# A place of its own in the written order for each step of a pair of batches, in a two-layer mixer with routed experts

## The reference

```python
for layer in (0, 1):
    xn = (x - mean(x)) / sqrt(var(x) + 1e-5)
    if layer == 0:
        xx = shift(xn) - xn                              # the token before, less this one
        mix = tanh((xn + xx * maa_x) @ w1)               # 5 groups of 32
        xw, xk, xv, xr, xg = (xn + xx * (maa[i] + mix[i] @ w2[i]) for i in range(5))
        r, k, v, g = xr @ Wr, xk @ Wk, xv @ Wv, silu(xg @ Wg)
        w = time_decay + tanh(xw @ d1) @ d2
        # per head, over time: y = r (S + u k v^T);  S = exp(-exp(w)) S + k v^T
        s = (groupnorm(y) * g) @ Wo
        f = sum over the 2 best of 8 experts: p_e * W3[e] (silu(xn W1[e]) * (xn W2[e]))
    else:
        s = concat_heads(softmax(q k^T / sqrt(8)) v) @ W_out
        f = shared(xn) + sum over the 2 best of 8 experts: expert_e(sigmoid(score_e) * xn)
    x = x + s * silu(f)
```

## Time and profile before

| what | value |
| --- | --- |
| median of 3 runs | 2736.35 us (2729.3 to 2741.03) |
| span of the profiled execution | 2756.3 us, 50388 instructions |
| TensorE, matmuls | 2327.5 us busy, 84% of the span |
| TensorE, weight loads | 1579.5 us, 57% |
| VectorE | 1609.7 us, 58% |
| ScalarE | 1350.3 us, 49% |
| GpSimd | 1237.6 us, 45% |
| 16 transfer engines | 31% of their time, 90 GB/s |

### The profile page before, as it was taken

How to read it: one execution, slowest core, us unless ns; L and a number is a source line. 1 busy time by engine, 2 the same in 40 slices (tenths; PEclk the granted TensorE clock), 3 DMA queues, 4 the chain that set the end, 5 groups by cost and what they waited for, 6 DMA issues and landing times. The chain is left out here.

```text
span 2756.3 us, 50388 instructions
## 1 busy us (share of the span) xinstructions
PE 2327.5 (84%) x16602; PEld 1579.5 (57%) x16602; DVE 1609.7 (58%) x3864; ACT 1350.3 (49%) x2485; POOL 1237.6 (45%) x1364
## 2 busy tenths in 40 slices
PE   1666889898998989898898989889898889998785
PEld 1553556566665656566565656556565656665363
DVE  2336465766657475665657465665647566665452
ACT  0222555455554546545554545545554555555453
POOL 3144435364633645444732646435643646323503
PEclk5768899999999999999999999999999999999897
DMA  3320223323333333323332333324333332321132
GB/s 104 111 75 12 68 91 95 106 73 111 98 100 89 99 99 99 94 77 111 101 103 82 99 93 97 107 75 121 100 90 93 96 102 85 110 72 41 53 107 68
DMA packets 308767, 248.27 MB, mean 90 GB/s; under 512 B 31040, under 2 KB 300064, under 8 KB 308512
## 3 DMA queue, kind: packets, MB, share of 16 engines
q1 hardware_dynamic: 292128, 211.46, 25.7%
q0 software_dynamic: 16384, 33.59, 4.1%
HBM read 195.77 MB, written 48.10 MB: 88 GB/s over the span
## 5 line engine op out<-in xcount | busy, mean ns | idle before, releaser
L1445 DVE TENSOR_REDUCE rowmax<-bank_s 128x1 f32<-128x512 f32 x1016 | 698.5, 687 | 565.6 <-PE bank_s L887 542.3
L1063 ACT ACTIVATE probs<-bank_st 128x512 f32<-128x512 f32 x992 | 589.4, 594 | 462.7 <-PE bank_st L902 431.9
L902 PE MATMUL bank_st<-qs,ks 128*128 128x512 f32 x992 | 512.6, 517 | 59.3 <-ACT probs L1063 58.0
L887 PE MATMUL bank_s<-ks,qs 128*128 128x512 f32 x1016 | 448.6, 442 | 93.8 <-DVE rowmax L1445 84.9
L1207 POOL DMA_INDIRECT yg<-ys_d,index x256 | 249.8, 976 | 260.7 <-issue 242.1
L902 PEld LDWEIGHTS bank_st<-qs,ks 128*128 128x128 f32 x992 | 191.5, 193 | 234.5 <-ACT probs L1063 140.6
L887 PEld LDWEIGHTS bank_s<-ks,qs 128*128 128x128 f32 x1016 | 197.0, 194 | 207.4 <-DVE rowmax L1445 173.6
L1329 DVE SCALAR_TENSOR_TENSOR hid<-hid,bank_h 128x512 f32<-128x512 f32 x224 | 148.6, 664 | 223.7 <-ACT hid L984 216.7
L916 PE MATMUL bank_pv<-probs,v 128*32 128x512 f32 x2048 | 253.8, 614 | 0.8 <-ACT probs L1063 0.8
L728 PEld LDWEIGHTS bank_h<-xT_sb,wbuf 128*128 128x128 f32 x1472 | 202.6, 202 | 27.9 <-issue 14.6
L1125 POOL TENSOR_TENSOR pause_sb<-ones_sb,power_sb 128x8 f32<-128x8 f32 x128 | 214.2, 1674 | 3.9
(11 more groups left out here) (245 smaller groups left out, 3659.4 us busy)
## 6 DMA issues: line engine op xcount, KB each, us to landing
wbuf<-up SPq DMA_DIRECT2D x368, 128.0 KB
wbuf<-gate SPq DMA_DIRECT2D x368, 128.0 KB
wbuf<-down SPq DMA_DIRECT2D x368, 128.0 KB
xs_sb<-xs_d SPq DMA_DIRECT2D x80, 256.0 KB
ys_d<-y_sb SPq DMA_DIRECT2D x80, 256.0 KB
xn<-x SPq DMA_DIRECT2D x16, 256.0 KB, 3.2
x<-x SPq DMA_DIRECT2D x16, 256.0 KB, 4.1
yg<-ys_d,index POOLq DMA_INDIRECT x256
```

What stands on the lines that cost most here:

```text
L887: mm(room(s, b)[:], qs[:, slot, q * P:(q + 1) * P], ks[:, slot, j, :], start=True, stop=True).then_inc(filled[b], 1)
L902: mm(room(s, b)[:], ks[:, slot, j, k * P:(k + 1) * P], qs[:, slot, :], start=True, stop=True).then_inc(filled[b], 1)
L1063: A(probs[:, tile % PRING, :], ps[:], ACT.Exp).then_inc(emptied[b], 1)
L1445: v.reduce_max(rowmax[:, h // HG % 2, NT * (h % HG) + q:NT * (h % HG) + q + 1], content(s, b)[:], AX).then_inc(emptied[b], 1)
```

## The change

Two tables are added, and two functions that read them. `MOVED` gives each single step of a pair of batches a number that is added to its due time on all engines: the key is the batch within the pair, the layer and the kind, and the list has one entry for each step of that kind. A second and a third dictionary hold what is added on top for the first and the last pair. `SHIFTED` adds a shift for each engine, layer and kind, again with an extra for the first and the last pair. `DRIFT` adds 0.0006 for each batch. The numbers in `MOVED` are mostly between -1 and 1, with some between -5 and 6; whole rows of layer 1's `gather`, `scatter` and `stack` move together. Nothing else is changed: the instructions, their operands, the banks and the waits are the same, but for the fill counts that are worked out from the new order.

```diff
-    return PERIOD * n + at
+    return PERIOD * n + at + moved(step)
+
+
+DRIFT = 0.0006
+MOVED = (
+    {
...
+        (1, 0, "wkvT"): [2.35], (1, 0, "wkvsum"): [-0.18], (1, 0, "yn"): [0.04],
...
+    },
...
+)
+SHIFTED = {
...
+    "dve": {
...
+        (1, "gate"): (-0.08, 0, 0), (1, "gather"): (-0.28, 0, 0), (1, "keys"): (-0.37, 0, 0), (1, "mrow"): (-0.02, 0, 0), (1, "normT"): (0.35, 0, 0),
...
+}
+
+
+def class_of(n):
+
+    return 1 if n < DUO else 2 if n >= B - DUO else 0
+
+
+def among(table, n, key, i, otherwise):
+
+    at = table[0].get(key, otherwise)[i]
+    return at + table[class_of(n)].get(key, otherwise)[i] if class_of(n) else at
+
+
+PLACES = [{} for i in range(DUO)]
+for places, steps in zip(PLACES, DUE):
+    for s in sorted(steps):
+        kin = [t for t in sorted(steps) if t[:2] == s[:2]]
+        places[s] = (kin.index(s), [0.0] * len(kin))
+
+
+def moved(step):
+
+    n = step[0]
+    i, still = PLACES[n % DUO][step[1:]]
+    return DRIFT * n + among(MOVED, n, (n % DUO, *step[1:3]), i, still)
+
+
+def shifted(engine, step):
+
+    every, *ends = SHIFTED[engine].get(step[1:3], (0, 0, 0))
+    return every + (ends[class_of(step[0]) - 1] if class_of(step[0]) else 0)
...
-    return sorted(PLAN, key=lambda s: due(s) + LATER[engine].get(s[2], 0.0))
+    return sorted(PLAN, key=lambda s: due(s) + LATER[engine].get(s[2], 0.0) + shifted(engine, s))
```

109 lines of the change are left out of this document (added).

## The result

The changed kernel takes 2609.87 us (median of 4 runs, 2604.09 to 2613.72) against 2732.82 us before (4 runs on the same chip, 2722.59 to 2741.03). The ratio is 0.9552, with a 95% interval of 0.9527 to 0.9577: 123 us less where 69 were forecast.

The account below looks back on a forecast made before the run. TensorE's idle time, 33.8 us a pair, bounds the kernel; 1.5 + 1.7 + 7.0 + 2.4 - 2.7 = 9.9 us a pair, times 7 is 69 off the 2736.35 median: 2670 us predicted, range 2622 to 2728 (8 in 10).

Parts of the forecast that it names:

- The row maximum behind combine: VectorE's queue: with wkvT behind the reduction, TensorE's 1.58 us bank_s wait goes; 1.5 us a pair.
- decay: ScalarE's queue: tanh ahead of two keys or an exponential shortens TensorE's wait between decay's halves; 1.7 us a pair.
- Short returns of the two banks: TensorE's order: fewer bank_s and bank_st matmuls follow their predecessor too soon; 7.0 us a pair, 4.9 visible.
- Places of other kinds: xT ahead of headsT, VectorE's statistics earlier, row maxima ahead of small operations; 2.4 us a pair.
- New waits: TensorE: one in 20 of 86 moved steps waits 0.6 us for its input; 2.7 us a pair back.
- the wait for wkvT: TensorE at L865: a new wait there would show the forecast wrong; wkvT was expected to fit by 0.3 us.
- GpSimd and SyncE at nothing: Norm behind three gathers, scatters, decays, lora and SyncE issues change places; costed at nothing, nothing gained.
- Half a pair for the start, 2 us for the end: Half a pair's gain added to 6.5 for the filling; the last 211.7 us left unchanged to 2 us.
- So there is little to be had: TensorE's granted clock, 0.98 in the six pairs, is nearly all at its upper level, so little gain there.
- The rule on the ports: VectorE and GpSimd lock shared SBUF ports: the collision moves to L1355, 0.6 us new wait a pair, 2674 us.
- more than is counted: Rival: an engine freed sooner frees its next bank sooner; 15 to 17 us a pair, 2617 to 2631; chance 0.13.
- the first rival: Waits only change place between the engines' queues; net under 2 us a pair, 2722 to 2736; chance 0.10.

Follow-up runs that it names:

- e13: The kernel before, unchanged, run again for a second profiled execution: 2731.26 us, ratio 1.0006.
- e9: The kernel before with only wkvT of each odd batch's layer 0 moved 2.35 us later: 2729.41 us, ratio 0.9983.
- e18: The changed kernel with only the move of wkvT in odd batches undone: 2610.52 us, ratio 0.9566.
- e10: The kernel before with only layer 0's decay moved earlier on ScalarE, ahead of keys and exponentials: 2728.86 us, ratio 0.9983.
- e5: The changed kernel with ScalarE's queue without its shifts: 2639.92 us, ratio 0.9657.
- e6: The changed kernel with VectorE's queue without its shifts: 2641.56 us, ratio 0.9674.
- e8: The changed kernel with the queues of GpSimd and SyncE without their shifts: 2625.05 us, ratio 0.961.
- e15: The changed kernel with both tables for layer 1 alone, layer 0 as before: 2723.30 us, ratio 0.9971.
- e3: The changed kernel with one table for all pairs, without extras for the first and last pair: 2612.15 us, ratio 0.9568.
- e11: The kernel before with matmuls of ones in TensorE's waits inside decay and for the norm of even batches: 2730.84 us, ratio 0.999.
- e17: e8 with three matmuls of ones ahead of the wait for mixin's input in even batches: 2623.68 us, ratio 0.9613.
- e16: The kernel before with the single moves of wkvT and of decay together: 2722.62 us, ratio 0.9976.

## Why the prediction was right or wrong

Right: what bounds the kernel (TensorE's idle time among the two banks), the sign, and what the places named look like afterwards. Wrong: the size, 9.9 us a pair where 19.1 came. The sum, sorted by what a trace can show (the 7.0 us of short returns count as 4.9 of waits and 2.1 of overlap, as the forecast split them):

| us a pair | forecast | measured, e13 against after |
|---|---|---|
| waits for the two banks, combine's included | 6.4 | 8.5 |
| waits inside decay | 1.7 | 1.6 |
| waits of other kinds | 2.4 | 3.1 |
| new waits, charged on top | -2.7 | none beyond what the three rows above are already net of |
| TensorE's busy time | 2.1 | 6.1 |

So the mechanism was right and three sizes were off: the short returns of the banks, the new waits, and above all the busy time, 4.0 of the 9.2 us missing. By the steps of the forecast:

- *The row maximum behind combine, 1.5 us.* The wait of 1.58 went and the add runs in 0.69, as said. As a term of a sum it fails: alone it gave under half (e9), and in the changed kernel its undoing costs nothing that the runs can tell (e18).
- *decay, 1.7 us.* Sized right as a wait: 1.6 us, 2.2 left where 2.1 was said. Alone it came back as 1.8 us of `bank_s` (e10).
- *Short returns of the two banks, 7.0 us, 4.9 of them visible.* This is the term that was mis-sized. The visible waits for the two banks fell by 8.5 us a pair, 7.0 of them without combine's. By starts of matmuls, the time that TensorE spends from each `soft` to its next matmul fell from 0.460 to 0.418 us, 5.3 us in 128, and from each `smax` by 5.5 us a pair: 10.8 us, where the two terms together had 8.5. The count looks at TensorE's row only and misses what the release of a bank waits for in the other two queues. The experiments refute it as a measure: e5, e6 and e8 have the count of the changed kernel and are 15 to 32 us slower, and e15 has a count 4.4 us worse than before and is faster.
- *Places of other kinds, 2.4 us.* A little too low; it is 3.1 net. The waits for the norm (1.5 us a pair), for the transfer of the experts' input (1.0) and for the transposed heads (0.8) are no longer in the list.
- *New waits, 2.7 us back.* They came, and more than said: 5.0 us a pair in front of 66 matmuls in six pairs, eleven a pair where four or five were taken. They are on the two banks (39 of the 66), at `bank_y` (0.5 us a pair), at the transposes behind `gT` (0.3) and at the router (0.2); one, of 0.6 us, is the wait for wkvT that the forecast named as a sign of being wrong. What the forecast missed is that 19.0 us of waits went against them. The count of short returns is net of most of this, so that charging 2.7 on top of it was the mistake: it is 19 of the missing 54 us.
- *GpSimd and SyncE at nothing.* Right for the norm behind three gathers, which no longer waits 9.77 us and delays nobody; wrong for the queues as a whole (e8, 15 us).
- *Half a pair for the start, 2 us for the end.* The 123 us are 6.5 pairs of 19.1, where the forecast took 7 and up to 2 us; 3.9 and 4.9 of them lie before and behind the six pairs. The tables of the first and last pair play no part that shows (e3).
- *"So there is little to be had" from the clock.* This was put at nearly nothing, and the runs don't bear it out. The lost clock went from 4.3 to 0.3 us a pair. In e11 and e17, 2.4 and 3.4 us less of it took 2.2 and 2.7 us off TensorE's busy time without the fillers. The pair became only 0.5 and 1.1 us shorter, but the fillers had put TensorE back by 1.35 and 1.4 us. If that delay counts in full, the clock gave about 1.8 and 2.5 us, and 4.0 us less lost clock would be worth about 3 of the 19.1; if it cost nothing, about 1. This is an estimate between two bounds; the timed runs (3.0 and 1.4 us) can't be told from nothing. The rest of the 6.1 us of busy time, about half, is in records that overlap more where the queue flows, as the forecast had it with 2.1. I infer that from the rows and haven't shown it apart.
- *The rule on the ports (the Trainium skill, "SBUF — State Buffer", section "SBUF: two separate sides").* The 1.41 us add beside GpSimd's subtraction became 0.69 without it, so far the trace agrees. The 0.6 us of new wait behind L1355 didn't come. That isn't against the page, which gives the ports to whichever of the two starts first: L1506 (the same line, now) starts 0.22 us before the subtraction, is overlapped by it for 0.47 us, and takes 0.69 us. It is GpSimd that pays: its subtraction takes 1.36 us behind L1506, and 1.04 for the odd batches, where it starts behind a row maximum, whose input is a bank. The forecast took the rule as a loss of VectorE's without asking who comes first.

```profile
1072.44 1.04 POOL L1289 TENSOR_TENSOR shiftT<-xnT 128x512 f32<-128x512 f32 x1 [4.27 <-DVE mixa L1573]
```

- *The base.* Taking 69 us off the median of the runs, not off the span, was right. But 2.6 of the 33.8 us of idle time a pair were waits of TensorE for its own matmuls that only that execution had.

The rival "more than is counted: one wait removed takes the next with it" gave 15 to 17 us a pair at a chance of 0.13; the measured 19.1 lies above even it. Its mechanism isn't what the runs show either. Single reliefs don't grow, they are in the main absorbed (e9, e10, e16, e18), which is the first rival's mechanism. What grows is the whole of the tables: places and shifts give 33 and 0 alone and 123 together, layer 0 and layer 1 give 41 and 6.

What stays open: which combinations of moves carry the 76 us that neither layer gives by itself. The reading that fits all runs is that a matmul on a bank needs the queues to agree (its own place on TensorE, that of the reduction or exponential that frees the bank, and that of what feeds it), so that moving one of them only moves the wait, as e10 shows for one place; but no run moved one bank's queues together and nothing else.

## What to carry to other kernels

When two or three in-order queues hand buffers to each other, the price of a single moved step is not a term of a sum: alone it tends to come back as the next wait, and within a whole new order it may be worth nothing, while the whole is worth more than the parts. So bound such a change from above by the idle time of the engine that bounds (31 us here, of which 13 went) and by what its busy time can lose (6 here), and don't charge new waits at a flat rate on top of a count that is net of them. Before summing from a trace whose span is off the median of the runs, look for what that one execution has alone. And when a wait is filled to learn what the clock costs, measure the filler first: one longer than the wait adds the delay that it was meant to price.

## What the runs showed of the hardware

- TensorE's waits for its own last matmul are absent from 19 profiled executions and come 22 times in the middle of one, up to 1.3 us each, 15.6 us in six pairs, with the same kernel. Its six pairs are 21 us longer than those of the second execution of that kernel. Why they came is open.
- In e8 the stretch of 5 us with a wait of 1.92 us had a granted clock of 0.94 and the next 0.50, the lower level (1.2 GHz), and the matmuls behind the wait had records of 1.83 and 2.07 us; in e17, with three matmuls of ones in that wait, it stayed at 1.00 and the records were 1.02 and 1.12. Of 3.4 us less lost clock a pair 2.7 showed in TensorE's busy time.
- A float32 matmul of ones with 512 columns is two records, and three of them take 2.75 to 2.85 us.
- GpSimd's 128x512 subtraction takes 1.04 us behind a row maximum that reads a bank, and 1.36 us behind an operation of VectorE with two SBUF inputs that started 0.22 us before it; VectorE's add that started 0.49 us after the subtraction took 1.41 us instead of 0.69.
